# Step sizes and row broadcasts of a selective scan as single-pass float32r products of high and low parts

## The reference, cut to what matters

```python
x_dbl = einsum('bdl,ed->bel', u, x_proj_w)          # 16 + 16 + 16 rows
dt_low, Bm, Cm = split(x_dbl, [16, 32], axis=1)
dt = softplus(einsum('brl,dr->bdl', dt_low, dt_proj_w) + dt_proj_b)
# per time step, for 16 states n:
state = state * exp(dt * A) + (dt * u) * B_n
y     = sum_n state_n * C_n
```

## Time and profile before

| | |
|---|---|
| median of 3 runs | 972.17 us (972.08 to 972.51) |
| span of the profiled execution | 970.2 us |
| what lies around the span | no time of its own is given for the profiled execution; median less span is 1.97 us |
| TensorE busy | 819.7 us (84%), 2770 matmul records |
| TensorE weight loads | 406.0 us (42%) |
| VectorE busy | 776.5 us (80%) |
| ScalarE busy | 661.0 us (68%) |
| GpSimd busy | 532.7 us (55%) |
| mean granted TensorE clock | 0.919 of full speed |

### The profile page before, as it was taken

The page is one execution under the profiler, slowest core; times in us unless marked ns, Lnnn a source line. Parts: engine busy times, 40 slices in busy tenths (PEclk is TensorE's granted clock), DMA queues, the critical chain, the costliest instruction groups (busy, mean ns, idle before and its releaser), DMA issues. The chain is left out here.

```text
span 970.2 us, 9341 instructions
## 1 busy us (share of the span) xinstructions
PE 819.7 (84%) x2770; PEld 406.0 (42%) x2810; DVE 776.5 (80%) x905; ACT 661.0 (68%) x984; POOL 532.7 (55%) x461
## 2 busy tenths in 40 slices
PE   6721247799799999999799999998899999898999
PEld 2210023354344344454344444444343444446887
DVE  4589997895989998985889998976899998964333
ACT  4699979673699963773599873772799863714442
POOL 0698786302899884212999882214998881012000
PEclk9755558799899999998899999999899999999999
DMA  8179982001299965301399963301599961201231
GB/s 299 20 136 218 272 197 46 1 1 44 44 202 235 237 139 141 109 2 43 61 218 239 234 137 109 109 1 44 114 221 209 236 143 53 109 1 44 87 109 66
DMA packets 46819, 119.57 MB, mean 123 GB/s; under 512 B 5793, under 2 KB 6945, under 8 KB 46257
## 3 DMA queue, kind: packets, MB, share of 16 engines
q0 software_dynamic: 16128, 58.73, 32.3%
q1 hardware_dynamic: 30640, 60.24, 18.4%
HBM read 56.03 MB, written 4.19 MB: 62 GB/s over the span
## 5 line engine op out<-in xcount | busy, mean ns | idle before, releaser
L1669 POOL TENSOR_TENSOR work<-du,bcast 128x1024 f32<-128x1024 f32 x128 | 352.3, 2780 | 32.5 <-ACT bcast L868 31.8
L1272 DVE TENSOR_TENSOR_SCAN pair<-pair,work 128x512 f32<-128x512 f32 x256 | 299.3, 1215 | 33.6 <-ACT pair L883 29.9
L883 ACT ACTIVATE pair<-dt,a_neg 128x512 f32<-128x512 f32 x256 | 165.7, 681 | 20.2 <-DVE work L1279 17.2
L654 PE MATMUL bank<-stage,ring 128*128 128x512 f32 x384 | 172.9, 593 | 5.7 <-ACT bcast L868 4.4
L1279 DVE TENSOR_TENSOR work<-pair,ccast 128x1024 f32<-128x1024 f32 x128 | 156.7, 1225 | 11.6
L1684 POOL DMA_DIRECT2D u<-work x112 | 122.0, 1089 | 35.7 <-DVE work L1279 15.8
L439 PE MATMUL bank<-xd,pick 128*128 128x512 bf16 x108 | 48.2, 446 | 82.4 <-ACT bcast L868 56.0
L654 PEld LDWEIGHTS bank<-stage,ring 128*128 128x128 f32 x384 | 71.8, 190 | 80.5 <-issue 70.9
L1655 POOL TENSOR_SCALAR fst<-fst 128x1 f32<-128x1 f32 x32 | 9.3, 290 | 169.9 <-DVE fst L1506 169.6
L668 PE MATMUL bank<-ring,stage 128*128 128x512 f32 x192 | 85.6, 594 | 1.7 <-ACT hx L1152 1.7
L439 PEld LDWEIGHTS bank<-xd,pick 128*128 128x128 bf16 x128 | 13.0, 102 | 140.1 <-ACT bcast L868 89.7
(11 more groups left out here) (169 smaller groups left out, 1501.5 us busy)
## 6 DMA issues: line engine op xcount, KB each, us to landing
u<-work POOLq DMA_DIRECT2D x112, 512.0 KB, 5.9
ring<-ffn_dram SPq DMA_DIRECT2D x120, 256.0 KB, 4.7
ring<-ffn_dram SPq DMA_DIRECT2D x16, 512.0 KB, 3.4
xres<-x_dram SPq DMA_DIRECT2D x4, 1024.0 KB, 5.4
stage<-w_dram SPq DMA_DIRECT2D x1, 4096.0 KB, 17.0
stage<-w_dram SPq DMA_DIRECT2D x4, 1024.0 KB, 7.5
out_dram<-stage SPq DMA_DIRECT2D x16, 256.0 KB, 2.1
ctxT<-ctxT_dram SPq DMA_DIRECT2D x4, 512.0 KB, 6.2
```

The lines of the kernel that those rows point to most:

```text
L654: last = pe.matmul(banks[2 + f % 2][:], piece(b, f)[:, k * P:(k + 1) * P], xnT[:, k, :], start=k == 0, stop=k == J - 1)
L883: act.activation(pairs[s % DECAYBUFS][:, q, :], dt[:, p * HALF + q, :], ACT.Exp, scale=a_neg[:, p * HALF + q, n:n + 1]).then_inc(s_decay, 1)
L1272: dve.tensor_tensor_scan(pair[:, q, :], pair[:, q, :], rows[:, q, :], 0.0, ALU.mult, ALU.add).then_inc(s_scan, 1)
L1669: pool.tensor_tensor(work[:, s % SCANBUFS, :, :], du[:, p * HALF:(p + 1) * HALF, :], bcast[:, n % 2, :].unsqueeze(1).broadcast_to([P, HALF ...
```

## The change

- `low_rank` now gives rank rows twice (0 to 31), B and C rows twice (32 to 95), rank rows twice again (96 to 127): the host array is the same, but `xpw` is loaded in two pieces.
- `low_rank_copy` is one activation, which writes all 128 rows rounded to float32r into `xsp`. `split` is one subtraction on rows 64 to 127: PSUM less `xsp`, rounded to float32r, so rows 64 to 127 hold the low parts. In `between` it stands ahead of `second(b,2)`.
- `dtw4` (128 rows) holds the high part of `dtw` at rows 0 and 96, its low part at 16 and 112, zeros between. A step-size product is one float32r product of 128 rows. It waits for `s_split` where it waited for `s_xd`.
- `pick_r` is `pick` in float32r with rows 96 to 127 zero. A broadcast is one float32r product. The first one waits for one step size where it waited for all four.
- At the start ScalarE rounds `dtw` (16 x 512), VectorE subtracts, GpSimd clears `dtw4` and issues four DMAs of 32 KB from attention scratch `attT`; VectorE makes `pick_r` in `gate_bias`. The load of `dtw` moves ahead of the other constants.

```diff
         consts = (
-            (xpw[:], xpw_d.rearrange("(k p) e -> p k e", p=P)),
-            (gates[:], gate_d), (dtw[:], dtw_d), (pick[:], pick_d), (ident[:], ident_d), (identb[:], identb_d),
+            (xpw[:, :, 0:96], xpw_d[:, 0:96].rearrange("(k p) e -> p k e", p=P)),
+            (xpw[:, :, 96:P], xpw_d[:, 0:2 * R].rearrange("(k p) e -> p k e", p=P)),
+            (gates[:], gate_d), (pick[:], pick_d), (ident[:], ident_d), (identb[:], identb_d),
...
+            sp.dma_start(dtw[:], dtw_d).then_inc(s_dtw, 16)
             for dst, src in consts:
...
                 if n == 0 and i == 0:
-                    pe.wait_ge(s_split, b + 1)
-                    pe.wait_ge(s_dt, b * J + J)
+                    pe.wait_ge(s_pick, 1)
+                    pe.wait_ge(s_dt, b * J + 1)
...
-                pe.matmul(banks[0][:], pick[:, i * NS + n:i * NS + n + 1].broadcast_to([P, P]), xd3[:],
-                          start=True, stop=True).then_inc(s_bc, 1)
+                pe.matmul(banks[0][:], in_parts(pick_r[:, i * NS + n:i * NS + n + 1]).broadcast_to([P, P]),
+                          in_parts(xsp[:]), start=True, stop=True).then_inc(s_bc, 1)
...
             def step_sizes(b, prev):
-                pe.wait_ge(s_xd, b + 1)
+                pe.wait_ge(s_dtw4, 4 * 16)
+                pe.wait_ge(s_split, b + 1)
...
-                    pe.matmul(banks[DT_BANKS[j]][:], dtw[:, j * P:(j + 1) * P], xd[0:R, :],
+                    pe.matmul(banks[DT_BANKS[j]][:], in_parts(dtw4[:, j * P:(j + 1) * P]), in_parts(xsp[:]),
...
-                act.activation(xd[:], banks[0][:], ACT.Copy)
-                act.activation(xd3[:], banks[0][:], ACT.Copy).then_inc(s_xd, 1)
+                act.activation(in_parts(xsp[:]), banks[0][:], ACT.Copy).then_inc(s_xd, 1)
...
+            act.wait_ge(s_dtw, 16)
+            act.activation(in_parts(dtw_high), dtw[:], ACT.Copy).then_inc(s_dtwhigh, 1)
             act.wait_ge(s_first, first_wait)
...
             def split(b):
                 dve.wait_ge(s_xd, b + 1)
-                tmp = x1n[:, 0, :]
-                dve_p.link(dve, b, dve.tensor_tensor(tmp, xd[:], xd3[:], ALU.subtract))
-                dve_p.link(dve, b, dve.tensor_copy(xd3[64:128, :], tmp[64:128, :]))
-                dve_p.link(dve, b, dve.tensor_tensor(tmp[96:128, :], tmp[96:128, :], xd3[96:128, :], ALU.subtract))
-                dve.tensor_copy(xd3[96:128, :], tmp[96:128, :]).then_inc(s_split, 1)
+                dve.tensor_tensor(in_parts(xsp[64:128, :]), banks[0][64:128, :], xsp[64:128, :],
+                                  ALU.subtract).then_inc(s_split, 1)
...
+                split(m)
                 second(b, 2)
-                split(m)
                 second(b, 3)
...
+            dve.wait_ge(s_dtwhigh, 1)
+            dve.tensor_tensor(in_parts(dtw_low), dtw[:], dtw_high, ALU.subtract).then_inc(s_dtwlow, 1)
             dve.wait_ge(s_first, first_wait)
             def gate_bias():
                 dve.wait_ge(s_const, const_wait)
+                dve.tensor_copy(in_parts(pick_r[:]), pick[:]).then_inc(s_pickc, 1)
+                dve.wait_ge(s_pickc, 1)
+                dve.memset(pick_r[96:128, :], 0.0).then_inc(s_pick, 1)
...
+            pool.memset(dtw4[:], 0.0).then_inc(s_zero4, 1)
...
+            pool.wait_ge(s_zero4, 1)
+            pool.wait_ge(s_dtwlow, 1)
+            for row, part in ((0, dtw_high), (R, dtw_low), (96, dtw_high), (96 + R, dtw_low)):
+                pool.dma_start(dtw4[row:row + R, :], part).then_inc(s_dtw4, 16)
             pool.wait_ge(s_const, const_wait)
```

More of the change, by code:

```diff
@@ L135, in program @@
         dtw = sb("dtw", [R, D])
+        dtw4 = sb("dtw4", [P, D])
+        pick_r = sb("pick_r", [P, 2 * NS])
         pch = sb("pch", [P, J, PC_N])
@@ L154, in program @@
         xd = sb("xd", [P, L])
-        xd3 = sb("xd3", [P, L], BF16)
+        xsp = sb("xsp", [P, L])
         attT = sb("attT", [P, J, D])
@@ L214, in down_load @@
             return 2 * FT - 1 - f if f < PIECES else 2 * FT + f - PIECES
+        dtw_high, dtw_low = attT[0:R, 0, :], attT[0:R, 1, :]
         def tail_slot(f):
@@ L256, in program @@
         s_split = sem("s_split")
+        s_dtw = sem("s_dtw")
+        s_dtwhigh = sem("s_dtwhigh")
+        s_dtwlow = sem("s_dtwlow")
+        s_dtw4 = sem("s_dtw4")
+        s_zero4 = sem("s_zero4")
+        s_pickc = sem("s_pickc")
+        s_pick = sem("s_pick")
         s_dtmm = sem("s_dtmm")
@@ L322, in program @@
         s_hlow = sem("s_hlow")
-        dve_p = Tally(sem("dve_p"), 2 * J + 3)
+        dve_p = Tally(sem("dve_p"), 2 * J)
         dve_m = Tally(sem("dve_m"), 4 * T)
```

## The result

| | before | after |
|---|---|---|
| median | 972.12 us (972.03 to 972.51, 4 runs) | 957.32 us (956.02 to 959.12, 4 runs) |
| span of the profiled execution | 970.2 us | 953.9 us |
| mean granted clock | 0.919 | 0.930 |

The ratio is 0.9835, 95% interval 0.9813 to 0.9857: faster by 14.8 us, where the forecast had 12.9; 957.3 us lies inside the range of 955.5 to 967.5.

A forecast was written before the change was run, and what follows sets the result against it. TensorE's stream was taken to bound the betweens, ScalarE the first scan, TensorE with ScalarE the gelu loop. Terms -12.6 - 3.2 + 2.9 = -12.9 us on 970.2, plus 1.97, gave 959.3 us; range 955.5 to 967.5.

The forecast's parts named there:

- Betweens, -12.6: Three betweens, step sizes to `attend(b,0)`: shorter products and no clock fall save 3.7, 5.3 and 3.6 us, sum 12.6.
- The new wait: Before `down1(b,3)`: TensorE waits for the second half of `h_copy`, starting at about 650.75 us; some 2.0 of 2.7 us kept.
- the clock's part: Three betweens: without any clock fall but with the old products, starts come 1.7, 3.4 and 1.7 us earlier, 6.8 of 12.6.
- the 0.76 us of idle time: Third between: TensorE stands idle 0.76 us from the step sizes' end to `down1(b,3)`, because `h_copy` ends later.
- The rival in which the clock falls all the same: Betweens and opening: clock still falls behind the step sizes, gain only 5.1 us, 967.1 us in all; chance 0.18.
- Opening, -3.2: Opening: GpSimd's first input moves from 32.76 to 29.5 us and, as the later engine, sets the 3.2 us gain.
- The upper bound, 4.4: Opening: the gain is 4.4 us if the decays, moving from 36.37 to near 32.0 us, decide.
- The rival of late transfers: Opening: the `dtw4` transfers come late and TensorE stalls once at 24 us, 1.7 us more, 961.0 us; chance 0.08.
- Broadcasts, +2.9: Gelu loop, slots 5 to 8 of three later scans: exposed float32r weight load costs 24 x 0.12 = 2.9 us.

The follow-up runs named there:

- run 1: Kernel before with its float32 step-size products kept but taking 128 rows, 112 weight rows zero: 964.80 us, ratio 0.9901.
- run 7: Changed kernel with its 128-row float32r step-size products each given four times over: 966.03 us, ratio 0.9940 to the kernel before.
- run 9: Changed kernel with down1's wait for the second half of the copied transposes moved ahead of its ninth product: 955.23 us, ratio 0.9809 to the kernel before.
- run 6: Changed kernel with float32r step-size products of 16 rows, each given four times over: 974.15 us, ratio 1.0021 to the kernel before.
- run 2: Changed kernel with float32r step-size products over the first 16 rows alone, one record each: 958.23 us.
- run 3: Changed kernel with the old float32 16-row step sizes and the float32 copy they need: 972.42 us, ratio 0.9991 to the kernel before.
- run 8: Changed kernel with `rates` moved to the start of ScalarE's program and 4 fillers in place of 12: 960.65 us.

## Why the prediction was right, and where it was off

**Betweens, -12.6.** Measured -12.85. The three starts of `attend(b,0)` moved by 3.51, 5.15 and 3.46 us against the step sizes; the rest is 0.12 us ahead of the step sizes in each between and 0.36 us behind `attend(b,0)` in the first. The new wait (650.75 in the forecast's frame, 1.67 us behind the step sizes) stands at 636.92 - 635.10 = 1.82 us. Run 1 measures the clock's part alone, 1.84 + 3.48 + 1.79 = 7.1 us (6.8 forecast), run 7 shows that a long group keeps the clock when it has 128 rows, and run 9 takes 0.8 us per between out of the new wait, which is the 0.76 us of idle time that the forecast named.

**The fall and its cause.** The forecast took it that the clock stays up because the group that came before each fall is gone, and it stayed up in all four places. Runs 6 and 7 show that the rows matter in a long group, run 2 that a short one does no harm; which of the two keeps the clock up in the changed kernel itself is not separated, since either was enough in these traces. The forecast leaned on four falls in four groups; runs 3 and 6 have falls in two of four (opening and one between) and three of four. So the 6.8 us are what this execution lost, not what every execution loses, and before's runs spread over 970.2 to 977.0 us in later rounds.

The rival in which the clock falls all the same rested on the rule of the Trainium skill ("TensorE: Matmul & The Clock Gate", Part 1) that an idle engine brings the clock down. Run 6 speaks against reading it as the only reason: the clock fell behind an engine busy 3.60 of 3.60 us with 16-row products. The measurement decides. The falls at the starts of the later scans do stand behind idle time: TensorE was busy 4.05 of the 8.10 us up to the fall at 663.1 us in the changed kernel.

**Opening, -3.2.** The step that was wrong is the choice of the engine: "GpSimd is the later one, so I take 3.2 us". GpSimd did come 3.03 us earlier, but the first scan is run by VectorE, whose first operation waits for ScalarE's decays, and these came 4.07 us earlier. `last_sum` is 4.25 us earlier. The upper bound, 4.4, was the better value. In eleven of the twelve traces `last_sum` comes 124.2 to 125.2 us behind the first scan operation, and 127.5 to 129.7 us behind GpSimd's first input (run 8 lies outside both). The forecast also read the first scan as ScalarE's, from one full row; over that whole scan before, VectorE stood idle in gaps of 7.1 us in all, ScalarE 11.2.

The transfers of `dtw4` were issued by 11.03 us; the page of the changed kernel has their median time to landing:

```profile
dtw<-attT POOLq DMA_DIRECT2D x4, 32.0 KB, 6.2
```

So they landed near 17 us, well ahead of the step sizes at 24.13, beside the 4 MB load. The rival of late transfers did not come.

**Broadcasts, +2.9.** Size and place were right: 0.12 us behind a wait, 7.84 us a period, 0.86 us a scan from the 7th to the 31st copy (2.6 in three), 2.3 us over three whole scans by the pooled traces. In the profiled pair alone it shows as +1.5, in the main because the stretch at low clock at the start of the second scan happened to be 3.4 us shorter after.

**Not forecast: the first turning, -1.1.** The same work ran in a shorter stretch, 26.59 to 25.51 us; the ten runs have 25.7 to 26.6. The page shows a low clock in these slices before and after; I did not test what sets its end and count the 1.1 us as spread. The median came out 2.0 us below the forecast; the opening's missing 1.05 us is one part of that, the rest lies within the spread of the runs.

## What to carry to other kernels

Look at the granted clock just behind narrow products: filling the unused rows with zeros cost the products no time and kept the clock up here (run 1), and so did making the group short (run 2). After shortening a step, look which wait ends last next; here it was the second half of a copy, and splitting that wait gave more than any work on the opening did. A product with a slower weight load (0.19 us here for float32r, 0.10 for bf16) pays for it where it stands behind a wait and that wait is what the loop hangs on: in slots 5 to 8, not in the first scan.

## What the runs showed that I had not expected

- The fall behind 16-row products is not certain: the same 3.6 us group kept its clock in the second between of run 6 and in the second and third of run 3.
- A group of 0.9 us with 16 rows brought no fall in any of four places (run 2).
- Executions of one kernel in the same rounds differ by up to 6.7 us for before (970.33 to 977.00) and 3.1 us for after, without any edit. Profiles that agree to 0.01 us in a between can differ by 1.9 us in the span.
- Making the first broadcast sooner made the whole slower (run 8). A 1.28 us table load that lost its cover took the gain away; the loss is in the main a first scan 1.6 us longer, whose cause stays open.
